# A two-layer attention and mixture kernel: front stage written out in one order, routing moved into it, and a narrow weight block handled in one pass

## The reference, cut to what matters

```
xn = layernorm(x)                                  # x: (2, 2048, 512)
q = xn @ Wq; lat = xn @ Wkv; k = lat @ Wk; v = lat @ Wv
s = windowed_attention(q, k, v) @ Wo               # window 128, 16 persistent keys, 16 heads
scores = sigmoid(xn @ gate_w)                      # 32 experts, 4 groups of 8
keep the 2 groups with the largest maximum; top 6 experts; weights = scores / their sum
expert_out = sum over the 6 of weight * (silu(xn @ w_gate[e]) * (xn @ w_up[e])) @ w_down[e]
shared = (silu(xn @ sw_gate) * (xn @ sw_up)) @ sw_down      # inner width 704
x = x + s * silu(expert_out + shared)
... a second layer: linear attention and a wide shared expert ...
```

## Time and profile before

| | |
|---|---|
| median of 3 runs | 4359.86 us (4357.02 to 4362.62) |
| the profiled execution's own time | 4356.47 us |
| its span in the profile | 4354.7 us |
| PE busy | 4047.8 us, 93% |
| DVE, ACT, POOL busy | 2142.3 us (49%), 1661.1 us (38%), 1359.5 us (31%) |
| HBM traffic | 384.36 MB read, 174.34 MB written |
| front, from 0 to the first DMA of the next stage | 322.7 us |
| route, from there to the first score | 62.5 us |

### The profile page before, as it was taken

The page is one execution under the profiler, slowest core; times in us unless marked ns, Lnnn a source line. Parts: engine busy times, 40 slices in busy tenths (PEclk is TensorE's granted clock), DMA queues, the critical chain, the costliest instruction groups (busy, mean ns, idle before and its releaser), DMA issues. The chain is left out here.

```text
span 4354.7 us, 69033 instructions
## 1 busy us (share of the span) xinstructions
PE 4047.8 (93%) x22805; PEld 3499.5 (80%) x22806; DVE 2142.3 (49%) x4182; ACT 1661.1 (38%) x3234; POOL 1359.5 (31%) x2020
## 2 busy tenths in 40 slices
PE   6984999989999999999997999995999999999998
PEld 5863777779989999998986888885788888788887
DVE  4447888744444444444444665654343333333333
ACT  2213777734434444444432443432332222222222
POOL 0003454445555555555552244444000000000000
PEclk9877999989999999999998999997999999999999
DMA  5767676555555565555654544533331331231321
GB/s 185 282 250 187 144 164 140 105 125 124 130 114 126 128 131 124 126 125 122 132 119 133 181 162 148 180 116 121 106 109 61 104 102 61 97 104 61 100 82 46
DMA packets 351911, 561.39 MB, mean 129 GB/s; under 512 B 33089, under 2 KB 198625, under 8 KB 347490
## 3 DMA queue, kind: packets, MB, share of 16 engines
q1 hardware_dynamic: 282770, 394.19, 30.0%
q0 software_dynamic: 68944, 164.62, 17.7%
HBM read 384.36 MB, written 174.34 MB: 128 GB/s over the span
## 5 line engine op out<-in xcount | busy, mean ns | idle before, releaser
L1250 POOL DMA_INDIRECT acc_d<-e_yw,e_to x208 | 335.9, 1615 | 287.0 <-ACT e_yw L1407 270.5
L2340 POOL DMA_DIRECT2D out<-d_res x32 | 17.3, 542 | 1306.2 <-DVE d_res L2571 1306.2
L2519 DVE TENSOR_TENSOR d_h<-d_sg,d_psU 128x512 f32<-128x512 f32 x144 | 99.0, 687 | 520.9 <-PE d_psU L107 462.6
L983 ACT ACTIVATE a_pr<-a_sm,a_nmax 128x272 f32<-128x272 f32 x512 | 263.8, 516 | 124.6 <-DVE a_nmax L1037 120.4
L1469 DVE TENSOR_TENSOR e_h<-e_sg,e_psU 128x352 f32<-128x352 f32 x208 | 108.2, 520 | 393.1 <-ACT e_sg L1420 390.5
L105 PE MATMUL e_psG<-e_gu,e_xT 128*128 128x352 f32 x832 | 289.2, 348 | 10.3 <-DVE e_xT L1461 9.9
L107 PE MATMUL e_psG<-e_gu,e_xT 128*128 128x352 f32 x832 | 271.6, 326 | 0.0
L106 PE MATMUL e_psG<-e_gu,e_xT 128*128 128x352 f32 x832 | 271.1, 326 | 0.0
L105 PE MATMUL e_psU<-e_gu,e_xT 128*128 128x352 f32 x832 | 270.6, 325 | 0.0
L106 PE MATMUL e_psU<-e_gu,e_xT 128*128 128x352 f32 x832 | 269.2, 324 | 0.0
L105 PE MATMUL e_psY<-e_wd,e_hT 128*128 128x512 f32 (+1 forms) x624 | 265.8, 426 | 1.2 <-DVE e_hT L1452 1.2
(11 more groups left out here) (432 smaller groups left out, 11909.8 us busy)
## 6 DMA issues: line engine op xcount, KB each, us to landing
d_gu_raw<-in_wgu SPq DMA_DIRECT2D x144, 512.0 KB, 3.3
qk_d<-f_qk SPq DMA_DIRECT2D x32, 1024.0 KB, 6.5
a_q<-qk_d SPq DMA_DIRECT2D x96, 256.0 KB
a_k<-qk_d SPq DMA_DIRECT2D x96, 256.0 KB, 4.4
e_rawgu<-in_w_gate SPq DMA_DIRECT2D x32, 704.0 KB, 6.0
e_rawgu<-in_w_up SPq DMA_DIRECT2D x32, 704.0 KB, 5.8
b_gu_raw<-in_wgu SPq DMA_DIRECT2D x40, 512.0 KB, 3.9
xT_d<-f_xT SPq DMA_DIRECT2D x16, 1024.0 KB, 13.6
```

What stands on the lines that cost most here:

```text
L983: act.activation(pr[half][:, h % HH, :], sm[s % SR][:, :], ACT.Exp, bias=nmax[s % SR][:, :], scale=-1.0, accum_out=rs[u % 2][:, h:h + 1]). ...
L1250: pool.indirect_dma_start(env.acc_d, bass.IndirectOffsetOnAxis(ap=to[:, :].bitcast(U32), axis=0), yw[:, :], None, compute_op=ALU.add).then ...
L2519: ins = dve.tensor_tensor(hv[q % 2][:, :], sg[q % 2][:, :], psU[:, :], ALU.mult)
```

## The change

- **Front:** all groups are written out in one order of items (`items`). The logits are now computed the other way round (R: gate weights stationary, 12 matmuls with 512 columns and 32 output rows), copied to SBUF and turned back by 4 small transposes. The order is R, W, Q, then T of the next group, then K and V. V is copied out by ACT alone. k has one staging buffer instead of two. x is loaded first, and the five weights go to buffers of their own.
- **Routing in the front:** DVE does the ranking and the choice of experts per group, GpSimd sums the one-hot tables, PE counts two matmuls of 128 columns per group; `phase_route` is gone.
- **Attend:** DVE forms the slots from the counts ahead of the loop (`first_slots`); the split of Wo moves into the loop at steps 12 and 14; the zeros of `acc_d` are written in 11 pieces with the loads of tiles 4 to 14.
- **Mix:** gate and up of the narrow block share one set of 12 matmuls into psG (up in rows 0 to 63, gate in rows 64 to 127; the host lays the columns accordingly), and the next gate waits for `h_ready`.

```diff
+    items = [("T", 0, j) for j in range(GT)]
+    for g in range(GROUPS):
+        items += [("R", g, 0), ("W", g, 0)] + [("Q", g, m) for m in range(4)]
+        items += [("T", g + 1, j) for j in range(GT)] if g + 1 < GROUPS else []
+        items += [("K", g, m) for m in range(4)] + [("V", g, j) for j in range(GT)]
...
-        qk = [sb(f"f_qk{i}", [P, 8, 2, G], F32R) for i in range(2)]
+        q = [sb(f"f_q{i}", [P, 4, 2, G], F32R) for i in range(2)]
+        k = sb("f_k", [P, 4, 2, G], F32R)
...
+            x_load(0)
+            for n in weights:
+                w_load(n)
+            x_load(1)
...
+            for g in range(GROUPS):
+                c = Chain(pool, hot_step, 2 * g)
+                pool.wait_ge(chosen, g + 1)
...
+                c(pool.tensor_tensor(hot[:, :, 0:3, :], hot[:, :, 0:3, :], hot[:, :, 3:6, :], ALU.add))
...
+            w_upper("wg")
+            w_upper("wkv")
             root(0)
...
+                if j == 0 and kind == "K" and g:
+                    act.wait_ge(k_out, 32 * g)
...
+            def groups_best(g):
+
+                dve.wait_ge(l_full, g + 1)
+                c(dve.tensor_scalar(lc[:, :, :, :].rearrange("p t g e -> p (t g e)"), psL[:, :], SIG_ONE, SIG_ZERO,
+                                    ALU.min, ALU.max))
...
+            stats(0)
+            variance(0)
+            w_lower("wg")
+            w_lower("wkv")
+            normalize(0)
+            w_lower("wq")
...
-            pe.wait_ge(w_used, len(weights))
...
+            turn(0)
+            for g in range(GROUPS):
+                x2 = lambda c, t: [xT[g % 2][h][:, c, t] for h in range(2)]
+                pe.wait_ge(lo_done, dve_count[place["T", g, GT - 1]])
+                weights_ready(g, "wg")
+                o = out(place["R", g, 0])
+                for c in range(KC):
+                    ins = mm3(pe, o[0:E, :], [wg[h][:, c, :] for h in range(2)], x2(c, slice(0, G)), c == 0, c == KC - 1)
...
+                    if m == 0 and g:
+                        count(g - 1)
+                if g + 1 < GROUPS:
+                    turn(g + 1)
+                pe.wait_ge(lo_done, dve_count[place["W", g, 0]])
...
-        phase_route(nc, env, place, first_loads, first_built, first_split)
...
+                if u in SUMS_AT:
+
+                    i = 3 * SUMS_AT.index(u)
+                    sp.dma_start(env.acc_d.rearrange("(i p) d -> p i d", p=P)[:, i:i + 3, :],
+                                 env.gu_raw0[:, 0:D].unsqueeze(1).to_broadcast([P, 3, D])).then_inc(sums_zero, 16)
...
-            dve.wait_ge(wo_hi, 1)
-            dve.tensor_tensor(wo[1][:, :, :], wraw[:, :, :], f(wo[0][:, :, :]), ALU.subtract).then_inc(wo_split, 1)
+            first_slots()
+            dve.wait_ge(mask_in, 64)
...
+                if s == WO_AT + 2:
+                    dve.wait_ge(wo_hi, 1)
+                    dve.tensor_tensor(wo[1][:, :, :], wraw[:, :, :], f(wo[0][:, :, :]), ALU.subtract).then_inc(wo_split, 1)
...
                     if q:
-                        pe.wait_ge(sg_ready, q)
+                        pe.wait_ge(h_ready if narrow(q - 1) else sg_ready, q)
+                elif narrow(q):
+                    return
...
+                    if narrow(q):
+                        ins = mm3(pe, psG[:, :], [wgt_both(q % 2, h, c) for h in range(2)],
+                                  [x2[g % 2][h][:, c, :] for h in range(2)], c == 0, c == KC - 1)
...
-                act.activation(sg[q % 2][0:k, :], psG[0:k, :], ACT.Silu).then_inc(sg_ready, 1)
+                act.activation(sg[q % 2][0:k, :], psG[gate_rows(q), :], ACT.Silu).then_inc(sg_ready, 1)
```

More of the change, by code:

```diff
@@ new lines, in phase_front @@
+        raws["wq"] = vst[1][:, :, :, :].rearrange("p j h d -> p j (h d)")
+        weights = {"wg": (env.gate_w, wg), "wkv": (env.Wkv, wkv), "wq": (env.Wq, wq), "wk": (env.Wk, wk), "wv": (env.Wv, wv)}
+        order = {n: i for i, n in enumerate(weights)}
+        w_in = {n: sem(f"f_{n}_in") for n in weights}
+        w_hi, w_split = sem("f_w_hi"), sem("f_w_split")
+        built, filled = sem("f_built"), sem("f_filled")
+        x_in = [sem(f"f_x_in{i}") for i in range(2)]
+        normed, var_ready, root_ready = sem("f_normed"), sem("f_var_ready"), sem("f_root_ready")
@@ new lines, in _ @@
+            pool.memset(ones[:, :], 1.0).then_inc(built, 1)
+            pool.memset(before[:, :], 1.0).then_inc(built, 1)
+            pool.memset(lower[:, :, :], 1.0).then_inc(built, 1)
+            pool.wait_ge(built, 10)
+            pool.affine_select(out=before[:, :], in_=before[:, :], compare_op=ALU.is_gt, fill=0.0,
+                               base=0, pattern=[[1, P]], channel_multiplier=-1).then_inc(built, 1)
+            pool.affine_select(out=lower[:, :, :], in_=lower[:, :, :], compare_op=ALU.is_gt, fill=0.0,
+                               base=0, pattern=[[1, NG], [-1, NG]], channel_multiplier=0).then_inc(built, 1)
@@ L270, in root @@
                 act.activation(rstd[:, :], var[:, :], ACT.Sqrt).then_inc(root_ready, 1)
-            def hi(g, b, more=True):
-                act.wait_ge(st_free, g + 1)
-                for j in range(ITEMS):
-                    if j == ROOT_AT and more:
-                        root(g + 1)
-                    if j == 4 or j >= 14:
-                        continue
-                    act.wait_ge(full, g * ITEMS + j + 1)
-                    act.activation(dest(b, j, 0), psum(b, j), ACT.Copy).then_inc(hi_done, 1)
@@ L519, in do @@
+            c = Chain(dve, step)
             def do(ins):
@@ L582, in _ @@
-            c(dve.tensor_copy(first_f[:, 1:E + 1], last[:, :]))
-            do(dve.tensor_scalar(first_f[:, E + 1:E + 2], last[:, E - 1:E], -3.0, None, ALU.add))
-            c(dve.tensor_copy(env.first[:, 0:E + 2], first_f[:, :]))
-            do(dve.tensor_scalar(base[:, :], first_f[:, 0:E], float(P), None, ALU.mult))
-            do(dve.tensor_tensor(base[:, :], base[:, :], start[:, :], ALU.subtract))
-            do(dve.tensor_tensor(run[:, :, :], run[:, :, :], cnt[:, :, :], ALU.subtract))
@@ L597, in _, with w_lower, stats @@
-            do(dve.tensor_scalar(odd_i[:, :], mid_i[:, :], 1, None, ALU.bitwise_and))
-            do(dve.tensor_scalar(env.first[:, E + 3:E + 4], odd_i[:, :], 1.0, None, ALU.add))
+            def w_lower(n):
+                dve.wait_ge(w_hi, order[n] + 1)
+                hi_, lo_ = weights[n][1]
+                dve.tensor_tensor(lo_[:, :, :], raws[n], f(hi_[:, :, :]), ALU.subtract).then_inc(w_split, 1)
+            def stats(g):
+                dve.wait_ge(x_in[g % 2], 16 * (g // 2 + 1))
+                for j in range(GT):
+                    c(dve.bn_stats(st[:, j, :], x_sb[g % 2][:, j, :]))
@@ new lines, in _ @@
+            w_lower("wq")
+            for j in range(GT):
+                lo("T", 0, j)
+            w_lower("wk")
+            w_lower("wv")
+            for g in range(GROUPS):
+                more = g + 1 < GROUPS
+                logits_out(g)
+                if more:
+                    stats(g + 1)
+                lo("W", g, 0)
+                if more:
+                    variance(g + 1)
+                lo("Q", g, 0)
+                if not more:
+                    groups_best(g)
+                    experts_best(g)
+                if more:
+                    normalize(g + 1)
+                lo("Q", g, 1)
+                if g:
+                    counts_out(g - 1)
+                lo("Q", g, 2)
+                if more:
+                    groups_best(g)
+                lo("Q", g, 3)
+                if more:
+                    for j in range(GT):
+                        lo("T", g + 1, j)
+                    experts_best(g)
+                for m in range(4):
+                    lo("K", g, m)
@@ L753, in phase_attend @@
         hits = sb("a_hits", [P, TOPK, E])
+        run_of = pr[1][:, :, :].rearrange("p h w -> p (h w)")
+        one_row = run_of[:, 0:TILES * E]
+        run = run_of[:, TILES * E:2 * TILES * E].rearrange("p (e t) -> p e t", e=E)
+        small = env.raw_gu0[:, :, :, :].rearrange("p c a m -> p (c a m)")[:, KC * D:]
+        ex = small[:, 0:TILES * TOPK].rearrange("p (t k) -> p t k", k=TOPK)
+        wsum, start, tot, nt, last, base, nt_i, nt_s = (small[:, n:n + E] for n in range(192, 192 + 8 * E, E))
+        first_f = small[:, 448:448 + E + 2]
+        mid_i, odd_i = (small[:, n:n + 1].bitcast(I32) for n in (496, 497))
+        nt_i, nt_s = nt_i.bitcast(I32), nt_s.bitcast(I32)
         slot = sb("a_slot", [P, TOPK])
```

691 lines of the change are left out of this document (335 added, 356 removed).

## The result

The kernel before took 4359.09 us in the median of four runs beside the changed one (4357.02 to 4362.62), the changed kernel 4222.31 us (4217.84 to 4223.39). The ratio is 0.9683, 95% interval 0.9667 to 0.9700: faster by 137 us, where 151 were forecast and 4182 to 4240 was the range. On a second chip the same two kernels gave a ratio of 0.9673 (0.9660 to 0.9686).

The account below looks back on a forecast made before the run. The front was held by PE, with half clock and idle, and DMA came close behind; PE bounded mix and attention. Savings 59.1 + 21.5 + 7.1 + 41.7 + 21.5 = 150.9 from 4359.9 gave 4209 us, own bounds 4195 to 4222, range 4182 to 4240.

Parts of the forecast that it names:

- Start, end, route: Earlier first logits save 21.5 us, shorter front tail 7.1, removed route stage 45.2 up to the first attention score.
- next stage's first DMA near 231: Sign in the new profile: the stage after the front issues its first DMA near 231 us.
- Front, 59.1: Seven group periods of the front shrink from 34.34 to 25.9 us, saving 59.1.
- the ring wait: In the front, V2 on PE waits about 0.9 us per group for DVE's K0 split to free a PSUM bank.
- once both are gone: Front's clock stays at 1.00 without the 2.37 us idle stretch and short matmuls; half clock had cost 5.2 us a group.
- The rule that was weighed: Skill's rule: bursts cut by waits are throttled repeatedly; applied to the front's 0.9 us wait, 4251 us, chance 0.07.
- Just under PE's 25.9: Front: DMA needs 25.0 us per group against PE's 25.9, so both bound it.
- rival 1: DMA sets the front's pace at 28.5 us a group, giving 4230 us; chance 0.17.
- Route's give-back: Attention gives back 2 us waiting for tile 1's loads and 1.5 for Wo's split inside the loop.
- Zeros at nothing: Zeros written in the attention loop cost nothing, hidden by SP's idle time; uncovered, up to 2.1 us each, 23 in all.
- Mix, 21.5: Mix: eight times 12 matmuls go, 2.76 us each; the gate's wait for the product is hidden by 1.7 us; 21.5 saved.
- Rival 5: DVE's chained routing steps bound the front and make the kernel slower, 4395 us at 1.6 us per step; chance 0.02.

Follow-up runs that it names:

- choice_late: Changed kernel with DVE's choice of experts moved behind the four K splits in the front; 4202.86 us, ratio 0.9644 to the kernel before.
- keys_first: Changed kernel with DVE taking the older group's keys ahead of the newer one's residuals at step 4 of each mix group; 4194.92 us, ratio 0.9628.
- late_turn: Changed kernel with x of the next group turned after V again, bringing back the gap ahead of the logits; 4220.92 us, ratio 0.9696.
- both_moves: Changed kernel with the choice of experts behind the K splits and the mix's keys ahead of the residuals; 4184.36 us, ratio 0.9607.
- zeros_twice: Changed kernel with 10 pieces of the attention loop's zeros, 7.9 MB, written a second time; 4214.30 us, ratio 0.9678.
- narrow_only: Kernel before with only the mix's narrow block put into one pass of 12 matmuls; 4336.48 us against 4354.54, ratio 0.9961.
- tile1_first: Changed kernel with both DVE moves (front's choice, mix's keys), plus Wo loaded behind tile 1's keys, values and queries; 4183.78 us, ratio 0.9600.
- small_logits: Changed kernel with the router back to 48 matmuls of 32 columns, x still turned early; 4264.06 us, ratio 0.9783.

## Where the prediction was right, and where not

The forecast (chance 0.54) is what happened; 4222 lies 13 us above its 4209 and at the end of its own bounds. By stages the mechanisms came as told; the misses are sizes, and one part is luck (the first score, below).

- **Start, end, route.** 21.5, 7.1 and 45.2 forecast, 21.9, 6.2 and 45.1 measured. The first score at 17.3, read from the rows of before, came at 17.45, but this is in part luck: the forecast had GpSimd done at 15.4 and the loads behind it as the last, and measured is GpSimd itself at 17.3, since its four casts of the persistent keys took 3.08 us in place of 1.42. The "next stage's first DMA near 231" doesn't follow from the forecast's own terms, which give 19.0 + 181.3 + 34.7 = 235; measured is 239.3.
- **Front, 59.1 against 55.4.** The term that was mis-sized is the ring wait: 0.9 us by counting DVE's queue, 1.24 measured as idle and 1.53 by what its removal gave (`choice_late`). PE's own work was put 0.3 too high (25.0, measured 24.70), which hides part of it: six periods of 26.23 instead of 25.9, 2 us. The other 1.7 is the first period, 27.64 instead of 25.9: ten of group 0's wide logits ran 0.43 us apart (18.69, 19.12) instead of 0.23, the pace of half clock. The windows read 1.00 there only because the trace has no clock entry before 22.8 us. The 16 transposes ahead of them took 3.65 us, where a group at full clock takes 1.91, so the clock had not risen yet. In `keys_first` the transposes are as slow, but the first entry of 1.00 is at 17.2 and the logits start at 18.57, 18.82 and 19.05, at full pace; the first period is 25.8. It is the clock's first rise that comes sooner or later, and the forecast had left it out.
- **The half clock.** The forecast took it away "once both are gone", and it went. Which of the two did it was open then: it is the short matmuls in every group (always with a wait of 1.0 us or more within 2 us ahead), the gap alone in 2 of 7. The rule that was weighed, of the Trainium skill (TensorE: Matmul & The Clock Gate, section on oscillation in real kernels), that matmul bursts cut by waits are throttled again and again, is not borne out by waits of 1.2 us (clock 1.00 in seven groups) and only in part by waits of 2.0 us: 2 of 7 in `late_turn`, and 2 to 5 of 6 in the mix.
- **DMA.** "Just under PE's 25.9" was right, and the bound is no higher than 24.7 us a group, with the queue at 100.6%. The chance of 0.17 for rival 1 was too high; the bursts of the earlier trace rows at full rate had said it.
- **Route's give-back, 3.5 against 4.0 systematic.** I had 2 us for tile 1's loads and 1.5 for Wo. It is the other way round: 1.1 of wait for the load (0.5 when it was moved) and the rest came with the split. The step left out is again the clock, which is at half for 10.2 us of the first tile and was at 1.00 before. A further 3.4 in this profile (loop slips and the last tile) is chance: it isn't there in `both_moves`, `zeros_twice` or `late_turn`.
- **Zeros at nothing**, named with the work that hides them: right, and shown with double the amount.
- **Mix, 21.5 against 16.7.** The block itself gave its 2.77 us in full in each group but the first, and the wait on the product stayed hidden. The step that failed was to leave out the falls of the clock at a wait of 2.0 us that was in the trace of before and that the change doesn't touch: 5 falls here against 2, 1.56 us each, 4.7 us.
- **Experts, 5.0 us more.** Nothing in the change reaches them. The stage took 1420.1 us in the kernel before and 1421.2 in `narrow_only`, 1421.1 to 1425.1 in the changed one and its variants (1421.1 in `tile1_first`, 1421.7 in `zeros_twice`). So up to 3 us of it may belong to the change and no run says by what. Left open.
- **Rival 5** (DVE's chained steps) had no weight: the ranking's small steps took 0.18 to 0.29 us, as counted.

## What to carry to other kernels

Turn a small product round so that the long side streams: here the fewer, wider matmuls saved more by keeping the clock up (2.7 us a group) than by their count (2.3). When PE's items are reordered to close a gap, look at what now stands ahead of each bank's release on the engine that empties them: a few lines moved on DVE gave 10.7 us in the front, and the same question at a wait that the change didn't touch gave 18.9. A wait of 2 us on PE was worth 2.3 to 3.8 us, since the clock may fall behind it; and work taken out of a stage where an engine idles (Wo's split) isn't free in the loop where it lands.

## What the runs showed of the hardware

With 48 matmuls of 32 streamed columns at 0.11 us each, back to back, with PE and weight load counted busy for the whole window, the granted clock went from 1.00 to 0.50 (2.4 to 1.2 GHz) in every group of `small_logits`, and it came back to 1.00 when 512-column matmuls had followed. A busy PE column is thus no sign that the clock will stay. Behind a gap of 2.0 us ahead of wide matmuls it fell in some places and not in others (2 of 7 in the front, 2 to 5 of 6 in the mix, there always the fourth and never the fifth), for about 1.56 us of lost time each; a gap of 1.2 us did it in none of the groups of the changed kernel. At the start of the program the clock first rose 17.2 us into one execution of the same front and 22.8 into another, worth 1.9 us. And SP's queue moved 382 GB/s over 140 us of mixed loads and stores (`choice_late`) without PE waiting for it.
